# Squared queries in two bf16 halves, turns in another order, two chunk buffers and a row bias with a pointer scalar, in a gated cross-attention kernel

## The reference

```
q = rmsnorm((layernorm(x) @ Wq) by head, gq)      # 16 heads, D = 128
k = rmsnorm((ctx @ Wk) by head, gk)
v = ctx @ Wv
attn = softmax(q k^T / sqrt(D))
x = x + tanh(g_xattn) * (attn v) @ Wo
x = x + tanh(g_ffn) * bitlinear(silu(bitlinear(ln(x), w_gate)) * bitlinear(ln(x), w_up), w_down)
wq = clip(round(w / mean|w|), -1, 1) * mean|w|    # each of the three weight matrices
```

## Time and profile before

| what | us |
|---|---|
| median of 3 runs | 2352.84 (2347.8 to 2357.62) |
| the profiled execution | 2351.92 |
| its span | 2350.1 |
| attention block, to the last residual | about 2062 |
| one pair, from residual to residual | 122.2 to 126.4 |

### The profile page before, as it was taken

The page is one execution under the profiler, slowest core; times in us unless marked ns, Lnnn a source line. Parts: engine busy times, 40 slices in busy tenths (PEclk is TensorE's granted clock), DMA queues, the critical chain, the costliest instruction groups (busy, mean ns, idle before and its releaser), DMA issues. The chain is left out here.

```text
span 2350.1 us, 45689 instructions
## 1 busy us (share of the span) xinstructions
PE 2215.9 (94%) x16187; PEld 1573.9 (67%) x16338; DVE 1837.9 (78%) x4171; ACT 1612.3 (69%) x3398; POOL 1273.9 (54%) x1623
## 2 busy tenths in 40 slices
PE   5889999999999999999999999999999999769999
PEld 3567777777776777777777777776767777534444
DVE  5788877787777787877777778777777777569997
ACT  4677777777776777666767777676767667546665
POOL 4555656565656555656666676767666655200000
PEclk9899999999999999999999999999999999989999
DMA  5776776666677776656676767676777665635665
GB/s 144 169 149 136 124 146 127 139 133 129 131 130 144 123 144 126 132 105 139 132 145 136 151 129 149 135 138 134 143 145 132 133 109 111 171 95 139 141 140 126
DMA packets 921748, 317.53 MB, mean 135 GB/s; under 512 B 864912, under 2 KB 882608, under 8 KB 921264
## 3 DMA queue, kind: packets, MB, share of 16 engines
q1 hardware_dynamic: 921520, 314.61, 66.6%
HBM read 82.09 MB, written 19.40 MB: 43 GB/s over the span
## 5 line engine op out<-in xcount | busy, mean ns | idle before, releaser
L1181 POOL TENSOR_TENSOR ksplit<-khat,ksplit 128x512 bf16<-128x512 f32 (+1 forms) x384 | 455.5, 1188 | 74.0 <-ACT ksplit L667 73.1
L893 DVE TENSOR_TENSOR khat<-keys_ps,krs 128x512 f32<-128x512 f32 (+1 forms) x384 | 263.4, 686 | 287.4 <-POOL krs L1175 287.2
L1175 POOL TENSOR_TENSOR krs<-kvar,minus_half 128x4 f32<-128x4 f32 (+1 forms) x384 | 387.1, 1008 | 32.0
L689 ACT ACTIVATE prob<-score_ps,nbias,qrs 100x361 f32<-100x361 f32 x512 | 328.6, 647 | 71.8 <-DVE nbias L911 70.4
L1172 POOL TENSOR_SCALAR kvar<-kss 128x4 f32<-128x4 f32 (+1 forms) x384 | 89.1, 232 | 531.9 <-DVE kss L883 530.0
L672 ACT ACTIVATE ksq<-keys_ps 128x512 f32<-128x512 f32 (+1 forms) x384 | 227.8, 596 | 188.5 <-PE keys_ps L25 188.4
L698 ACT ACTIVATE psplit<-prob,rden 100x361 bf16<-100x361 f32 x512 | 304.3, 595 | 64.9 <-DVE rden L917 64.2
L923 DVE SCALAR_TENSOR_TENSOR psplit<-prob,rden,psplit 100x361 bf16<-100x361 f32 x512 | 317.5, 629 | 4.2 <-ACT psplit L698 0.6
L901 DVE TENSOR_REDUCE nmax<-score_ps 100x1 f32<-100x361 f32 x512 | 268.3, 524 | 54.5 <-PE score_ps L25 54.3
L667 ACT ACTIVATE ksplit<-khat 128x512 bf16<-128x512 f32 (+1 forms) x384 | 240.5, 626 | 98.0 <-DVE khat L893 97.3
L24 PE MATMUL keys_ps<-wk_split,ctxT 128*128 128x512 bf16 (+1 forms) x768 | 293.8, 383 | 6.8
(11 more groups left out here) (132 smaller groups left out, 5323.1 us busy)
## 6 DMA issues: line engine op xcount, KB each, us to landing
stage<-in_ffn SPq DMA_DIRECT2D x96, 256.0 KB, 3.2
ctx_raw<-in_ctx SPq DMA_DIRECT2D x31, 256.0 KB, 3.5
xin<-in_x SPq DMA_DIRECT2D x32, 200.0 KB
res_rows<-in_x SPq DMA_DIRECT2D x32, 200.0 KB
x_rows<-res_rows SPq DMA_DIRECT2D x32, 200.0 KB
xin<-x_rows SPq DMA_DIRECT2D x25, 256.0 KB, 2.7
xres<-x_rows SPq DMA_DIRECT2D x25, 256.0 KB, 3.0
out<-xres SPq DMA_DIRECT2D x25, 256.0 KB, 2.0
```

The source lines that it names most:

```text
L689: act.activation(prob[:, h, :], score_ps[h % 2][0:SQ, 0:SK], ACT.Exp, bias=nbias[:, b, h:h + 1], scale=qrs[:, v // 2 % 2, r:r + 1], accum_ ...
L893: dve.tensor_tensor(khat[0:KV[t], k, :].rearrange("p (h d) -> p h d", h=G), keys_ps[k][0:KV[t], :].rearrange("p (h d) -> p h d", h=G), rs, ...
L1175: pool.tensor_tensor(krs[0:KV[t], k, :], kvar[0:KV[t], k, :], minus_half[0:KV[t], 0:G], ALU.pow).then_inc(krs_done, 1)
L1181: pool.tensor_tensor(ksplit[0:KV[t], t, 1, :], khat[0:KV[t], (u + t) % 2, :], ksplit[0:KV[t], t, 0, :], ALU.subtract).then_inc(k_lo_done, 1)
```

## The change

**Squares.** ACT squares each half of the queries twice, once into an f32 buffer of half the former size (`queries_square`) and once into bf16 (`queries_square_hi`); POOL subtracts (`query_squares_lo`, new). `query_squares` is 16 bf16 matmuls of one column with 128-column weights (the slices run over into the next columns, and the unused rows of the result are not read). yT lies in the same space.

**Order.** `two_turns` has another order on all four engines, and `shared_uses` follows it: squares stand behind the values and the last key tile, the second mixed product directly behind the first, the four projections together. `turn_x` has the values between its halves.

**Chunks.** `load_chunk` fetches one turn ahead into one of two buffers (stage slots 0 and 3); the rounded chunk lies in slot 2. The own stage slots are four instead of five. `weight_chunk` and `round_chunk` stand elsewhere in their turns.

**Context.** `load_ctx` is issued earlier (at the end of turns 2 and 6), and the three `split_ctx` steps of a turn stand together.

**Row bias.** tensor_tensor of two columns becomes tensor_scalar with a pointer scalar.

```
-    OWN_STAGES = 5
+    OWN_STAGES = 4
...
-        w_raw, w_out = stage[:, 0, :], sb("w_out", [P, CHUNK], BF16)
+        w_raw, w_out = [stage[:, 0, :], stage[:, 3, :]], stage[:, 2, 0:CHUNK // 2].bitcast(BF16)
...
             def load_chunk(i, u):
+                i, u = (i, u + 1) if u < UNITS else (i + 1, 1)
                 n, m = sum_chunk_of(i, u), tern_chunk_of(i, u)
...
+                    if m is not None:
+                        sp.wait_ge(w_summed, min(c - 1, MATRICES * CHUNKS))
+                        if m > 1:
+                            sp.wait_ge(w_rounded, m - 1)
+                    elif n > 1:
+                        sp.wait_ge(w_summed, n - 1)
...
-                        last = pe.matmul(ps[0:SQ, b * G + h:b * G + h + 1], qsq[:, h, b * SQ:(b + 1) * SQ],
-                                         ones[:, 0:1], start=True, stop=True)
+                        out, hi, lo = ps[:, b * G + h:b * G + h + 1], h * QT + b * SQ, (G + h) * QT + b * SQ
+                        pe.matmul(out, qsq_split[:, hi:hi + P], ones[:, 0:1], start=True, stop=False)
+                        last = pe.matmul(out, qsq_split[:, lo:lo + P], ones[:, 0:1], start=False, stop=True)
...
-                dve.tensor_tensor(nbias[:, b, h:h + 1], nmax[:, b, h:h + 1], qrs[:, v // 2 % 2, r:r + 1],
+                dve.tensor_scalar(nbias[:, b, h:h + 1], nmax[:, b, h:h + 1], qrs[:, v // 2 % 2, r:r + 1], None,
                                   ALU.mult).then_inc(nbias_done, 1)
...
             def queries_square(i, u, k):
...
+                if started(i * (NG * QD) + (u + 3) // 2 * QD + k):
+                    eng.wait_ge(q_sqlo_done, i * (NG * QD) + (u + 3) // 2 * QD + k)
+                act.activation(qsq[:, :, :], ps, ACT.Square).then_inc(q_sq_done, 1)
...
+            def query_squares_lo(i, u, k):
...
+                pool.tensor_tensor(qsq_lo[:, heads, :], qsq[:, :, :], qsq_hi[:, heads, :],
+                                   ALU.subtract).then_inc(q_sqlo_done, 1)
```

292 lines of the change are left out of this document (158 added, 134 removed).

## The result

The changed kernel takes 2399.3 us, median of 4 runs (2395.48 to 2403.51), against 2350.6 before: 1.021 times as long, 95% interval 1.0186 to 1.0234. The prediction was 2379, slower, range 2315 to 2418. The profiled execution took 2403.51 us, its span is 2401.7.

The account below looks back on a forecast made before the run. PE was taken to bound the kernel, busy 2215.9 of 2350.1 us. From 2351.92 us: squares -32, other waits -12, clock where x is turned -27, rounding chunks +91, summing pairs +7, giving 2379 us, range 2315 to 2418.

Parts of the forecast that it names:

- the chunk's road through SP: In the six rounding pairs, key transposes queue on SP behind the late-rounded chunk's store and the next load: +91 us.
- three signs of being wrong: Rounding pairs under 125 us, PE's wait at the value products above 3 us a pair, or squares again taking 1.3 us.
- six-transpose turn: Turn where SP issues three context transposes ahead of three key ones; PE waits 7.4 us for the third key transpose.
- The summing pairs: In six pairs that sum w_ffn, SP waits for ACT's chunk sum; only one turn is late, 1.2 us: +7 us.
- The squares: On PE, 16 bf16 products replace eight f32 ones in each of 64 groups, 0.5 us less each: -32 us.
- Where x is turned: Value products between the x turns break the low-activity stretch, so its low clock is gone: -27 us; new wait 1.8 us.
- The other waits: PE's waits fall to 2.6 us a pair against 3.4 before: -12 us over 15 pairs (-30 to +30).
- The row bias: On DVE, a column times a pointer scalar saves up to 80 us of DVE but brings nothing on PE.
- (1): Rival: shorter tail on DVE and POOL, only six-transpose turns wait, +33 in place of +91, 2321 us; chance 0.15.
- (2): Rival: SP's wait for the rounding doesn't reach PE at all, 2288 us; chance 0.10.
- (3): Rival: clock low once a pair (+27) and one-column products at the old pace (+32), 2438 us; chance 0.10.
- (4): Rival: the rounding wait is about two thirds of that counted and eats the gain, some 2353 us; chance 0.12.

Follow-up runs that it names:

- a_store_late: Changed kernel with chunk store and load behind the next turn's three key transposes on SP, and a second rounded-chunk buffer; 2270.71 us, ratio 0.967.
- a_xlo_early: Changed kernel with the low part of the first turned x moved on DVE ahead of one low part of the probabilities; 2380.88 us, ratio 1.0137.
- a_tt: Changed kernel with the row bias alone put back to a product of two columns in SBUF; 2476.24 us, ratio 1.0523.
- a_late_xlo_tt: Changed kernel with later chunk store and load, earlier low part of turned x, and the row bias back to a two-column product; 2336.74 us, ratio 0.9944.
- a_x_old: Changed kernel with the squares, only where x is turned, back between the first turned x and the values; 2420.22 us, ratio 1.0293.
- b_x_waits: Kernel before, with DVE's second mixed low part, second layernorm and low part of turned x moved earlier where x is turned; 2328.2 us, ratio 0.9909.

## Why the prediction was right, point by point

**The sign** came from one term, the chunk's road through SP, and that term is shown: taking two DMA issues out of the way gives back 129 us, 123.5 of them in the six rounding pairs (forecast 91, bounds 33 to 120, so it lies a little above the upper bound). The walk for an ordinary turn was close, by the rows shown above. From the end of keys v+2 on PE to the last low part it forecast 7.8 us and 8.7 passed (from the squares at 1210.37 to 1219.09), rounding with the step to SP 1.5 and 1.75, SP's third issue and its landing 6.9 and 6.9 (1220.84 to PE's start at 1227.71). PE waited 2.76 us in the place shown, against 1.8. None of the three signs of being wrong came: rounding pairs take 140 us, PE's wait at the values is 2.1, the squares take 0.40. But PE waited for keys 20 times and for the context 12 times in these pairs, and the long waits were not the ones foreseen.

**What was too small in it** is of three kinds. First, the context: at turn 5 too PE asked for context transposes that stood behind a store, and waited 2.0 to 3.8 us for them (0.3 to 1.9 in pairs without rounding), which the forecast did not have. Second, the place of the long wait: 7.4 us were forecast for the third kT of the six-transpose turn; PE waited 5.7 us for the context itself, and when it came to the scores the keys had landed. The walk had followed SP's list to its end and not asked which of the six PE takes first. Third, the clock: 15 us were forecast for the low clock in rounding pairs. The low time there is 85.3 us against 20.5, so half of 65, about 32 us. It fell 19 times there, not only after the six long waits. Together the six pairs have, against the kernel before, 83 us more of waits and 32 of low clock, less 23 for 24 groups of squares: +92 where +87.7 was measured.

**The summing pairs.** +7 was forecast. They take 119.9 us in the mean, the two full pairs without any chunk 120.0 and 118.2, and a_store_late gained 4.2 us in the six. The size was about right, as far as so small a difference can tell.

**The squares.** -32 was forecast, and undoing them costs 30. That is right by accident. The step that took the part of a load that scales with the clock, 0.05 us, as the price of a record was wrong: a record takes 25 ns, not 53, and the group 0.40 us, while each load still lasts 0.10 us; the loads overlap. But of the local 55 us in the fifteen pairs 25 were lost to waits, to the clock and to what stays open, which the sum had not charged.

**Where x is turned.** -27 for the low clock was forecast as gone in whole. In the seven pairs it fell from 23.9 to 10.2 us, a gain of 7 of 12. The new wait was forecast at 1.8 us and is 2.09, for the reason given (DVE's order), as a_xlo_early shows. After that wait the clock still falls in some pairs; with 0.95 us it does not.

**The other waits** (-12, called the softest part) did not come. In the seven pairs PE waited 16.5 us before and 23.7 after: 14.6 at the turned x (9.7 before), 9.1 for context and key transposes (none before), and the 6.8 that it had waited for DVE elsewhere are gone. The seven pairs add up: +7 of waits, -7 of low clock, -27 of squares against -25.5 measured. Most of the row bias is hidden in these waits: with two columns PE waits 48.9 us in the seven pairs (a_tt).

**The row bias.** "DVE is idle 22%, so it brings nothing on PE" was the step that failed worst: -25 on the kernel before, -77 in the changed one. The reasoning by a mean hid it. 314 ns is 160 for most and up to 1118 for some, the long ones stand in chains that PE waits for, and the change makes more of them. One reason, argued and not shown, why the total was still near: the pairs without rounding had been forecast by a walk with undisturbed durations, which is what the pointer scalar gives them. Without it they take 124.3 us (a_tt), no gain at all.

**How much of the number was luck.** Undone one at a time in the changed kernel, the chunk's road is worth +129 us, the row bias -77, the squares -30: +22 of the +49 measured. Such terms do not strictly add, but that leaves some +27 for all the rest (the order, the context's place, the chunk buffers, the turned x), where the prediction had -39. Its misses of 31 us on the road and the summing pairs, of -77 on the row bias and of 66 on the rest nearly cancelled. So the sign rests on a mechanism that is shown, and the nearness of 2379 to 2399 is in good part luck. The order and the place of the context's loads and splits were never put back alone, so their price is open.

**Of the rivals**, (1) and (2), that fewer waits or none would reach PE, are refuted by the waits in all six pairs. (3), the squares without gain and the clock low once a pair, is refuted by the rows of the squares (0.40 us); its low clock came in three of the seven pairs without rounding and several times in each rounding pair. (4) failed on the size alone.

## What to carry to other kernels

In a queue that several kinds of work share, look at what stands behind a wait, not at the wait: the store of a chunk that is read back 170 us later at the earliest held up transposes that PE asked for 6 us after their keys were ready, and moving store and load three entries down the list gave 129 us. When an instruction is moved later on one engine, move its store and the next load past whatever is urgent, and give it a second buffer so that the wait is not passed back. A tiny DVE operation on two SBUF operands beside a busy GpSimd need not be tiny; read its maximum, not its mean, and give one operand as a pointer scalar where it is one value per partition.

## What the runs showed of the hardware that was not expected

- A product of two 100x1 columns lasted up to 2.04 us: it starts 0.11 us into a POOL power of 1.0 us and waits for the following POOL subtraction too (45 such in a_late_xlo_tt, all 108 to 112 ns behind the start). Others that start elsewhere in such a POOL power took 0.15 to 0.20, and so did 12 that start 107 to 118 ns into one, so the point in time alone is not what decides. What does was not found out.
- bf16 products of one column with 128-column weights follow each other every 25 ns, weight load included, although each load lasts 0.10 us; the f32 ones every 85 ns per record.
- In the seven pairs without rounding, the granted clock fell to 1.2 GHz for 3.4 us after a single wait of 2.1 us in three (the changed kernel), and in none with 0.95 us (a_xlo_early); after one of 2.27 us it fell in five, in three of them for 6.8 us (a_x_old). In the kernel before, 55 us of waits went with 58 us of low clock, some 29 us of time; b_x_waits took 10 us of waits and 34 of low clock away.
